# Attention heads: where the softmax is normalised, and how its maximum enters

## The reference

```python
x = x + jnp.tanh(g_xattn[0]) * _L0_xattn_ref(_layernorm(x), ctx_2048, mask, norm_w, wq, wk, wv, wo, wg)
x = x + jnp.tanh(g_ffn[0]) * _L0_ffn_ref(_layernorm(x), weight, bias)      # ternary weights, 8-bit rows
x = x + jnp.tanh(g_xattn[1]) * _L1_xattn_ref(_layernorm(x), ctx_2048, ctx_2048)
...
# _L0_xattn_ref: 16 heads of 32
x = rmsnorm(hidden_states, norm_w)
q, k, v = x @ wq.T, memory @ wk.T, memory @ wv.T          # each (B, 128, 16, 32)
attn = softmax(where(mask, q k^T * 32**-0.5, -inf))       # rows that are masked throughout give 0
out = (attn v) @ wo.T
return sigmoid(x @ wg.T) * out
```

## Time and profile before

| | us |
|---|---|
| median of 3 runs | 1397.67 (1394.35 to 1404.95) |
| profiled execution | 1401.04 |
| its span | 1399.3 |
| TensorE busy, share of the span | 1238.7 (89%) |
| VectorE | 719.3 (51%) |
| ScalarE | 553.9 (40%) |
| POOL | 426.3 (30%) |

### The profile page before, as it was taken

How to read it: one execution, slowest core, us unless ns; L and a number is a source line. 1 busy time by engine, 2 the same in 40 slices (tenths; PEclk the granted TensorE clock), 3 DMA queues, 4 the chain that set the end, 5 groups by cost and what they waited for, 6 DMA issues and landing times. The chain is left out here.

```text
span 1399.3 us, 25475 instructions
## 1 busy us (share of the span) xinstructions
PE 1238.7 (89%) x7821; PEld 1041.0 (74%) x7822; DVE 719.3 (51%) x1443; ACT 553.9 (40%) x1430; POOL 426.3 (30%) x504
## 2 busy tenths in 40 slices
PE   6998999999996599789987896799999989999992
PEld 6876777777774377556766675689999878999992
DVE  5666655655655599854667532433234543434330
ACT  4543444444542388632111011433334543434340
POOL 1101211211212556520035601134444433344442
PEclk9999999999998699889999998899999999999996
DMA  9000000000000111322000202455446655545456
GB/s 319 24 22 12 17 1 18 17 1 17 1 2 1 46 42 41 115 88 73 1 0 1 92 30 77 143 140 137 76 80 139 182 124 143 137 82 131 88 137 165
DMA packets 53881, 103.62 MB, mean 74 GB/s; under 512 B 5127, under 2 KB 20999, under 8 KB 53751
## 3 DMA queue, kind: packets, MB, share of 16 engines
q1 hardware_dynamic: 38182, 65.78, 14.2%
q0 software_dynamic: 15632, 36.97, 13.9%
HBM read 75.99 MB, written 30.93 MB: 76 GB/s over the span
## 5 line engine op out<-in xcount | busy, mean ns | idle before, releaser
L1703 PE MATMUL t_H<-m_W,t_xT 128*128 128x352 f32 x1632 | 286.6, 332 | 15.8 <-DVE m_W L1781 14.1
L1703 PEld LDWEIGHTS t_H<-m_W,t_xT 128*128 128x128 f32 x1632 | 268.2, 193 | 18.1 <-DVE m_W L1781 14.6
L1670 POOL DMA_INDIRECT acc_d<-t_ys,t_sid x68 | 109.4, 1609 | 284.6 <-ACT t_ys L1732 200.7
L1748 ACT ACTIVATE t_sl<-t_H 128x352 f32<-128x352 f32 x68 | 31.5, 464 | 174.6 <-PE t_H L1703 174.6
L597 ACT ACTIVATE pr<-pr 128x128 f32<-128x128 f32 x256 | 76.1, 299 | 55.3 <-DVE pr L758 53.9
L62 PE MATMUL t_Y<-m_W,t_hT 128*128 128x512 f32 (+1 forms) x207 | 88.6, 428 | 9.9 <-DVE t_hT L1826 6.8
L1802 DVE TENSOR_TENSOR t_h<-t_H,t_sl 128x352 f32<-128x352 f32 x68 | 35.6, 523 | 106.3 <-ACT t_sl L1748 105.7
L1732 ACT ACTIVATE t_ys<-t_Y,t_wcol 128x512 f32<-128x512 f32 x69 | 47.4, 687 | 95.5 <-PE t_Y L64 88.1
L1824 DVE TENSOR_TENSOR t_hT<-t_TH,t_hT 128x256 fp32r<-128x256 f32 x68 | 28.8, 423 | 106.5 <-ACT t_hT L1769 105.3
L64 PE MATMUL t_Y<-m_W,t_hT 128*128 128x512 f32 (+1 forms) x207 | 82.6, 399 | 0.0
L63 PE MATMUL t_Y<-m_W,t_hT 128*128 128x512 f32 (+1 forms) x207 | 82.3, 398 | 0.0
(11 more groups left out here) (411 smaller groups left out, 3237.3 us busy)
## 6 DMA issues: line engine op xcount, KB each, us to landing
m_r<-in_L_ffn_w_dram SPq DMA_DIRECT2D x26, 704.0 KB, 5.0
m_r<-in_L_ffn_w_dram SPq DMA_DIRECT2D x13, 512.0 KB, 6.8
aCX<-in_ctx_dram SPq DMA_DIRECT2D x20, 256.0 KB, 2.6
rows_d<-before_w SPq DMA_DIRECT2D x17, 256.0 KB, 2.0
CT<-in_ctx_dram SPq DMA_DIRECT2D x8, 512.0 KB, 3.7
X<-in_x_dram SPq DMA_DIRECT2D x4, 1024.0 KB, 13.2
acc_d<-X SPq DMA_DIRECT2D x4, 1024.0 KB, 4.2
m_r<-in_L_ffn_sw_dram SPq DMA_DIRECT2D x4, 704.0 KB, 5.5
```

The costliest lines, as they stand in the source:

```text
L1670: pool.indirect_dma_start(out=m["acc_d"][:, :], out_offset=bass.IndirectOffsetOnAxis(ap=sid[:, b:b + 1], axis=0), in_=ys[:, b, :], in_offs ...
L1703: x_ = pe.matmul(bk[b % 2][:, 0:I], xT[:, b % 2, jx, k, :], W13[:, jw, k, j, :], start=k == 0 and jx == jw, stop=k == KC - 1 and jx == 1)
```

## The change

The maximum is no longer subtracted by VectorE. VectorE turns it into `neg`, minus the scaled maximum (held from below, so that a row masked throughout gives zeros and not ones), and ScalarE takes `neg` as the bias of the exponential, which now reads the score bank itself. A new step `nr` per four heads holds the sums from below and inverts them on VectorE, and POOL multiplies the exponentials in place by the inverses, ahead of their transposes. The steps `rc`, `bc` and `on`, the bank `REC` and the tile `o` go; `O` gets a second bank, and `oT` reads it. The score banks are free again when the exponentials have read them (`p_exp`), no longer with the subtraction. The words of the plan are put in another order.

```diff
-        TILED = ("xT", "cT", "v", "g", "rc", "bc", "on", "oT", "oP", "st", "sf", "sx", "nm", "mk", "u", "uT", "fm")
+        TILED = ("xT", "cT", "v", "g", "oT", "oP", "st", "sf", "sx", "nm", "mk", "u", "uT", "fm")
...
-                f"Sa.0 xT.2 Sb.0 sm.0 sm.1 v.0 st.-2 st.-1 cT.2 ra.-1 xT.3 {d[0]} g.0 rb.-1 pT.0 cT.3 q.1.0 rd.-1 Sa.1 pT.1 Sb.1 "
-                f"sm.2 sm.3 mk.4 q.1.1 u.-2 {d[1]} pv.0 q.1.2 sf.-4 sf.-3 pT.2 uT.-2 u.-1 {d[2]} q.1.3 Sa.2 pT.3 rc.0 Sb.2 sm.4 sm.5 "
...
+                f"Sa.0 xT.2 Sb.0 sm.0 sm.1 v.0 st.-2 st.-1 nr.0 cT.2 nr.1 ra.-1 xT.3 {d[0]} g.0 rb.-1 cT.3 pT.0 rd.-1 "
+                f"Sa.1 pT.1 Sb.1 sm.2 sm.3 mk.4 q.1.0 sf.-4 sf.-3 q.1.1 nr.2 u.-2 {d[1]} nr.3 q.1.2 pv.0 uT.-2 u.-1 {d[2]} q.1.3 pT.2 "
...
# gpsimd
+                    elif kind == "nr":
+                        pp = pr[:, t % 2, :, :]
+                        pool.wait_ge(inverse, 2 * t + 2)
+                        pool.tensor_tensor(pp, pp, rec[:, t % 2, :].unsqueeze(2).to_broadcast([P, HQ, S]), ALU.mult)\
+                            .then_inc(p_norm, 1)
# tensor
-                            pe.wait_ge(p_exp, t + 1)
+                            pe.wait_ge(p_norm, t + 1)
...
-                            wait(pe, s_out, 4 * t)
+                            wait(pe, p_exp, 2 * t)
...
-                    elif kind == "bc":
-                        pe.wait_ge(o_norm, 2 * t + 1)
-                        wait(pe, r_out, t)
-                        for j in range(KC):
-                            for r in range(HQ):
-                                at_ = col_of(j, r)
-                                i = pe.matmul(REC[r * HD:(r + 1) * HD, j * S:(j + 1) * S],
-                                              rec[:, t % 2, at_:at_ + 1].to_broadcast([P, HD]), identF[:, :],
-                                              start=True, stop=True)
# scalar
+                        wait(act, t_fill, at(T_KINDS, ("pT", t - 2)))
                         for slot in range(HQ):
-                            pp, at_ = pr[:, t % 2, slot, :], t % HQ * HQ + slot
-                            i = act.activation(pp, pp, ACT.Exp, scale=SCALE0, accum_out=sums[:, t // HQ % 2, at_:at_ + 1])
+                            i = act.activation(pr[:, t % 2, slot, :], SC[t % 2][:, slot * S:(slot + 1) * S], ACT.Exp, scale=SCALE0,
+                                               bias=neg[:, t % 2, slot:slot + 1], accum_out=sums[:, t % 2, slot:slot + 1])
...
-                        act.activation(oT[:, 0, :, :].rearrange("p k t -> p (k t)"), o[:, :], ACT.Copy).then_inc(o_hi, 1)
+                        act.activation(oT[:, 0, :, :].rearrange("p k t -> p (k t)"), O[t % 2][:, :], ACT.Copy).then_inc(o_hi, 1)
# vector
-                        dve.tensor_tensor(pr[:, t % 2, :, :], bk, mx[:, t % 2, :].unsqueeze(2).to_broadcast([P, HQ, S]),
-                                          ALU.subtract).then_inc(s_out, 1)
+                        wait(dve, p_exp, t - 1)
+                        dve.tensor_scalar(neg[:, t % 2, :], mx[:, t % 2, :], MASKED / 10, -SCALE0, ALU.max, ALU.mult).then_inc(s_out, 1)
+                    elif kind == "nr":
+                        dve.wait_ge(p_exp, t + 1)
+                        wait(dve, p_norm, t - 1)
+                        dve.tensor_scalar(some[:, t % 2, :], sums[:, t % 2, :], 0.5, None, ALU.max).then_inc(inverse, 1)
+                        dve.wait_ge(inverse, 2 * t + 1)
+                        dve.reciprocal(rec[:, t % 2, :], some[:, t % 2, :]).then_inc(inverse, 1)
```

More of the change, by code:

```diff
@@ L169, in attention_heads_and_ternary @@
         pT = sb("pT", [P, 2, HQ, S])
-        mx = sb("mx", [P, 2, HQ])
-        sums, rec = sb("sums", [P, 2, NH]), sb("rec", [P, 2, NH])
-        o = sb("o", [P, D])
+        mx, neg = sb("mx", [P, 2, HQ]), sb("neg", [P, 2, HQ])
+        some = sb("some", [P, 2, HQ])
+        sums, rec = sb("sums", [P, 2, HQ]), sb("rec", [P, 2, HQ])
         oT = sb("oT", [P, 2, KC, S], F32R)
@@ L185, in attention_heads_and_ternary @@
         T, M, SC = bank("T", 2), bank("M", 2), bank("SC", 2)
-        O, REC = bank("O", 1)[0], bank("REC", 1)[0]
+        O = bank("O", 2)
         mask_f = dg[0:NB, :]
@@ L221, in steps @@
                         continue
-                elif kind in ("sm", "pT"):
+                elif kind in ("sm", "nr", "pT"):
                     nums[0] += NQ * g
@@ L290, in attention_heads_and_ternary @@
         s_half, s_fill, s_out, p_exp, pv = (sem(n) for n in ("s_half", "s_fill", "s_out", "p_exp", "pv"))
-        o_norm, r_out, o_hi, o_lo = (sem(n) for n in ("o_norm", "r_out", "o_hi", "o_lo"))
+        inverse, p_norm, o_hi, o_lo = (sem(n) for n in ("inverse", "p_norm", "o_hi", "o_lo"))
         added, biased, q_step, f_step = (sem(n) for n in ("added", "biased", "q_step", "f_step"))
         U_STEPS, F_STEPS = 6, 8
-        RING = SC + [O, REC]
-        def col_of(j, r):
-            return (j // 2 * 2 + r % 2) * HQ + r // 2 * 2 + j % 2
-        def ctx_after(eng, s):
-            wait(eng, t_fill, at(T_KINDS, s))
+        RING = SC + O
         with nc.Block() as block:
@@ L525, in _ @@
                             pe.wait_ge(m_dve, at(BY_DVE, ("v", b)))
-                            wait(pe, o_norm, 2 * b)
+                            wait(pe, o_lo, b - 1)
                         for jj in range(2):
@@ L728, in _ @@
                         dve.wait_ge(m_fill, mf)
-                        wait(dve, pv, at(PV, ("pv", 2 * t - 1)))
+                        wait(dve, pv, at(("pv",), ("pv", 2 * t - 1)))
                         dve.tensor_scalar(va[:, :, :], M[(mf - 1) % 2][:, :].rearrange("p (h d) -> p h d", h=NH),
```

41 lines of the change are left out of this document (12 added, 29 removed).

## The result

The changed kernel takes **1407.2 us** (median of 20 runs, 1398.9 to 1411.4) where the kernel before takes 1401.4 (20 runs, 1394.4 to 1407.1): ratio **1.004, 95% interval 1.0022 to 1.0058**. It is slower, by less than the 1% named in the prediction; the forecast was 0.6% faster, and 1407 lies outside the range.

The account below looks back on a forecast made before the run. TensorE, busy 361 of 384 us, was taken to bound the heads stage. Broadcasts -14.1, waits +12.8, clock -5.0 and two first-group waits -2.0 gave -8.3 us, so 1389.4 us; range 1372 to 1403.

Parts of the forecast that it names:

- POOL beside VectorE: Heads stage: VectorE's SBUF operations slow beside POOL's; counted once, 0.9 us in `u.1`; by the exclusive-lock rule 5 us more.
- Part 4, the clock: TensorE's low clock behind long waits: gone in second and last group, half gone in the first, -5.0 us.
- Part 2: Softmax: VectorE some 20 us lighter but no bound, worth nothing alone; exponentials longer at 0.37 us; POOL's added work fits.
- Part 3: New step order, walked through a group's eight slots: TensorE waits 8.5 us instead of 5.3, +12.8 us in four groups.
- Part 1: Heads stage: 16 broadcast matmuls of 0.88 us each leave TensorE, all on the path, -14.1 us.
- C: Rival: POOL becomes a slot's bound; gain gone at 1.42 us per multiplication, 1427 us at 1.9; chance 0.10.

Follow-up runs that it names:

- e4: Kernel before with only the maximum entering as the exponential's bias, order and broadcast matmuls kept; 1385.2 us, ratio 0.989, heads stage ends at 456.6.
- e9: Kernel before with the bias alone, in the changed kernel's order, reciprocals and broadcast matmuls placed as before; 1390.5 us, ratio 0.996, heads stage ends at 462.1.
- e1: Changed kernel without POOL's 64 multiplications, only the semaphore passed on; heads stage ends at 462.1 us against 479.4, whole time not comparable.
- e6: Changed kernel with `pv.7` moved ahead of `k.2.3` at each group's end; 1410.6 us, ratio 1.008, heads stage ends at 482.7.
- e3: Changed kernel's softmax and normalising with the steps in the order of the kernel before; 1434.2 us, ratio 1.025, heads stage ends at 504.2.

## Why the prediction was wrong

The stage ends 9.0 us later instead of 8.3 earlier. One path from before to the changed kernel, by runs that differ in one thing each: bias -13.9 (e4), order +5.5 (e9), broadcasts out and reciprocals in +0.1 (e1), multiplications +17.3 (changed): **+9.0**. Each term is known to some 3 us only, the +0.1 therefore as "small"; the medians of the two ends of the path are 5.8 apart. In another sequence the parts would be priced otherwise (the order is worth +5.5 with broadcasts and -24.8 with POOL).

- **The step that failed: "POOL beside VectorE. I have counted it once, in `u.1` (0.9 us)."** POOL's multiplications cost 17.3 us: 4.9 where their result is late, the rest through VectorE, which they hold, and the low clock behind it. I had asked where POOL's result was late and found it nearly nowhere, which was right for the groups with a next group behind them; in the last one it was wrong by a wait of 2.6 us. I had the rows that mattered, `axn` at 1514 ns for 546, and `fu<-fu`, which ends at 60.21 us, 0.28 behind POOL's at 59.93; I read only that it grew by less than POOL's rest. And I did not ask which VectorE instructions each of the 64 multiplications would lie beside, and what stands behind them in VectorE's queue. Against named waits: `pT.0` 1.9 us (2.15 by the loads) for 0.8, `uT.1` 1.75 for 1.1. At `uT.1`, `fu<-X` took 1.43 us for 0.55 and `fu<-fu` 1.07 for 0.49, both beside POOL.
- The Trainium skill ("SBUF — State Buffer", section "SBUF: two separate sides") has the loser blocked for the other's whole instruction, for VectorE operations in a fast mode or with two SBUF inputs. I gave that 5 us more. The trace agrees with the rule beside POOL's operations of 512 elements (ends within 0.03 us of POOL's in the fences above); beside POOL's power of 0.7 us, `some` took its usual 0.17. By the rule and my own list the sum would still have been 12 us short, since it was applied in two places of a group and without the clock.
- **Part 4, the clock, -5.0: wrong in sign.** The wait at `uT.0` went, as forecast, but the one at `pT.0` took its place, and the granted clock was 0.53 over 6 us of the second group and 0.71 over 7 of the third. Without multiplications slot 1 is 2.6 and 1.6 us shorter in these groups. How much of that a wait of 2 us costs is chance in part: e6 has the same wait in the second group and no low clock behind it, and in the kernel before the wait of 2.8 us before `uT.0` stands in three groups, with a low clock behind it in the second alone. So -5.0 took as given what one execution happened to show. Two forecasts hung on one wait: I had said that waits of at most 1.5 us would leave the clock alone, and the waits were longer.
- **Part 2, "no bound, so that alone is worth nothing": wrong**, -13.9 us (e4). My own view showed TensorE waiting for `u.0`; I gave that wait to the order in part 3, while lighter work on VectorE shortens it too. This error leans the other way; with part 2 sized right I would have forecast about 1375 and been further off.
- **Part 1, -14.1 us: paid in the steady groups, and lost again in the others.** The `REC` rows are gone and a steady group gains 2.3 us rather than 3.5 (e9 to e1), since TensorE's waits grow from 5.1 to 6.2 us. Over the stage e9 and e1 are equal. What the first and last group lose stands beside a low clock in e1; whether the reciprocals ahead of the transposes bring that about is not shown.
- **Part 3** was right in sum: TensorE's waits in the third group are 7.3 us for 4.7 before, where I had 8.5 for 5.3. Spared matmuls and waits would make that group 100.9 us; it takes 103.9, and slot 1 with its low clock is the only place on record for the rest. The list was near in the middle slots; `oP.3` waits 1.53 us for the halves of `oT.3` where I said 0.8. Slots 0 and 7 wait longer than forecast, slot 1 does not wait at all at its low clock.
- **The rivals.** C (POOL bounds a slot) had the sign but not the mechanism: the multiplication took 1.08 us, under its limit of 1.42, and C's waits are found in the old order (e3) and once in the last group. No rival had VectorE held up by POOL as its mechanism, though a row for it stood in my list.

What stays open: how much of the 17.3 us the low clock costs by itself. The four slots named at e1 hold 7.2 us, but the length of the low clock differs between executions with the same waits, and only one execution of each kernel shows its clock. A direct test would need the clock held fixed, or profiles of many executions.

## What to carry to other kernels

Moving work to an idle engine is free only if that engine doesn't stop a busy one: list what each moved instruction will lie beside, and what is queued behind that. An engine with a 60% busy share can still be the last to arrive at two places in a group, so that lighter work on it pays there (14 us here). Price a mechanism together with its order: the same order cost 5.5 us with one way of normalising and gave 24.8 with the other, and the best of both kernels came only when the order was written for the waits that the trace shows (1374.5 us, 1.7% under before). And a low clock seen behind a wait in one execution is no fixed price of that wait: look at it in more than one run before you put it into a sum.
